# Softmax shift as the bias of eight exponentials a group, in the second and fourth of four cross-attentions

## The reference

```
L0: x = x + MHA(LN(x), LN(ctx)), 8 heads of 32; then a state scan over the 1024 rows (silu), plus a row of program weights
L1: attn = softmax(where(causal, q k^T / 8, -inf)), 16 heads of 64; x = attn v @ wo + bo + x
L2: scores = where(mask == 0, -1e9, q k^T / 4); e = exp(scores - max) * mask; probs = e / (sum e + 1e-9), 16 heads of 16
    x = LN(probs v @ Wo.T + bo + x)
L3: attn = softmax(where(xa_mask, -max_float, q k^T / 4)), 16 heads of 16; x = x + attn v @ proj; x = x + gelu(LN(x) @ fc1) @ fc2
```

## Time and profile before

| | |
|---|---|
| median of 3 runs | 1384.22 us (1378.32 to 1384.23) |
| the profiled execution | 1379.43 us, its span 1377.7 us |
| PE, PEld busy | 97%, 82% of the span |
| DVE, ACT, POOL busy | 66%, 49%, 41% of the span |

### The profile page before, as it was taken

One profiled execution on the slowest core, in us unless ns is written; L12 is line 12 of the kernel. 1 busy time (PEld: TensorE's weight loads), 2 busy tenths in 40 slices (PEclk: granted clock), 3 DMA queues, 4 the chain that ended last, 5 costly groups with the idle time before them and its releaser, 6 DMA issues.

```text
span 1377.7 us, 22993 instructions
## 1 busy us (share of the span) xinstructions
PE 1334.6 (97%) x8763; PEld 1123.6 (82%) x8763; DVE 902.5 (66%) x2204; ACT 676.7 (49%) x1497; POOL 558.7 (41%) x700
## 2 busy tenths in 40 slices
PE   6999999999999999999999999999999999899999
PEld 4889987777788788878888888779877887788778
DVE  4778772787755867575667556775677467746771
ACT  3667766134555453545444535446344643464444
POOL 4455432016613552454246311472156216621661
PEclk9999999999999999999999999999999999999999
DMA  5133502200000000000000001000000000000000
GB/s 148 39 82 124 165 24 81 62 10 1 1 16 16 1 9 9 16 1 9 1 9 1 24 4 30 0 1 13 19 1 1 17 16 1 1 5 12 1 1 16
DMA packets 48362, 34.10 MB, mean 25 GB/s; under 512 B 22076, under 2 KB 45435, under 8 KB 48251
## 3 DMA queue, kind: packets, MB, share of 16 engines
q1 hardware_dynamic: 46919, 32.44, 8.2%
q10 hardware_dynamic: 1332, 0.17, 0.1%
HBM read 23.26 MB, written 8.39 MB: 23 GB/s over the span
## 4 chain that ended last, share of the span: by engine, by line
PE 87%; DVE 5%; POOL 4%; ACT 2%; issue 1%; ACTq 0%; DMA 0%; SPq 0%; DVEq 0%
PE ps L886 11%; PE ps L876 10%; PE ps L836 10%; PE ps L855 8%; PE ps L932 8%; PE ps L943 8%; PE ps L846 6%; PE ps L896 6%; PE ps L802 5%; PE ps L785 5%; PE ps L1037 2%; PE ps L1050 1%; POOL pr L1607 1%; POOL pr L1621 1%; PE ps L924 1%; PE ps L905 1%
## 5 line engine op out<-in xcount | busy, mean ns | idle before, releaser
L1582 POOL TENSOR_TENSOR rstd<-mv,halfneg 128x1 f32<-128x1 f32 x192 | 107.5, 562 | 343.6 <-DVE mv L1317 342.3
L1163 ACT ACTIVATE pr<-pr 128x616 f32<-128x616 f32 x224 | 160.1, 716 | 167.5 <-DVE pr L1356 87.2
L1621 POOL TENSOR_TENSOR pr<-mx,pr 128x616 f32<-128x616 f32 x128 | 156.4, 1223 | 207.9 <-DVE mx L1351 207.2
L1167 ACT ACTIVATE pr<-ps 128x512 f32<-128x512 f32 x224 | 132.7, 596 | 157.3 <-PE ps L855 157.1
L855 PE MATMUL ps<-ident,pr 128*128 128x128 f32 (+1 forms) x1120 | 161.1, 277 | 8.3 <-ACT pr L1163 4.8
L886 PEld LDWEIGHTS ps<-vtab,pr 128*128 128x128 f32 (+1 forms) x1280 | 153.5, 191 | 13.2 <-ACT pr L1167 9.1
L886 PE MATMUL ps<-vtab,pr 128*128 128x102 f32 (+1 forms) x1280 | 161.2, 274 | 2.3 <-ACT pr L1167 1.1
L855 PEld LDWEIGHTS ps<-ident,pr 128*128 128x128 f32 (+1 forms) x1120 | 126.9, 140 | 35.1 <-ACT pr L1163 10.0
L876 PE MATMUL ps<-vwo,pr 128*128 128x256 f32 (+1 forms) x640 | 148.9, 381 | 0.0
L1415 DVE TENSOR_TENSOR xt<-xt,ps 128x256 f32<-128x256 f32 x192 | 79.7, 416 | 104.1 <-PE ps L896 48.4
L836 PE MATMUL ps<-wk,tt 128*128 128x308 f32 x512 | 145.2, 425 | 0.7 <-ACT tt L1142 0.7
(11 more groups left out here) (200 smaller groups left out, 2361.5 us busy)
## 6 DMA issues: line engine op xcount, KB each, us to landing
out_dram<-xt SPq DMA_DIRECT2D x64, 128.0 KB, 1.7
xt<-in_x_dram SPq DMA_DIRECT2D x32, 128.0 KB, 2.7
xt<-out_dram SPq DMA_DIRECT2D x32, 128.0 KB, 2.1
fc<-in_L_xattn_fc_w_dram SPq DMA_DIRECT2D x2, 1024.0 KB, 5.6
wk<-in_L_xattn_wkv_dram SPq DMA_DIRECT2D x4, 512.0 KB, 5.0
front<-in_L_xattn_wkv_dram SPq DMA_DIRECT2D x4, 512.0 KB, 6.5
wo<-in_L_xattn_wo_dram SPq DMA_DIRECT2D x1, 1024.0 KB, 5.2
kb<-in_L_xattn_wq_dram SPq DMA_DIRECT2D x1, 1024.0 KB, 5.1
```

The costliest lines, as they stand in the source:

```text
L1163: ac(v, v, ACT.Exp, scale=-ATTN[key[0]].scale).then_inc(done["expo"], 1)
L1167: ac(pr[:, run.lane, 0:4 * P], bank(run.lane, 0), ACT.Copy).then_inc(done["pturn_main"], 1)
L1582: p.tensor_tensor(rstd[:, n:n + 1], mv[:, n, 1:2], halfneg[:, :], ALU.pow).then_inc(done["rstd"], 1)
L1621: p.tensor_tensor(p8, mx[:, run.lane, :].unsqueeze(2).to_broadcast([P, HG, KEYS]), p8, ALU.subtract).then_inc(done["below"], 1)
```

## The change

In L1 and L3 the subtraction is gone as a step of its own. The tables of keys are stored negated and scaled (`wk_sb` and `k_sb` multiply by -1/8 and -1/4), the masks add a large positive number instead of a negative one, and `rowmax` takes the minimum of the negated scores. `expo` then does eight exponentials of 77 columns, one a head, exp(least - score), where `least` is a column of `mx` given as bias. In L1 each of the eight also writes the sum of its row to a new small buffer `total`, and `rowsum` is dropped. L1's exponential reads PSUM directly; L3's reads `pr`, in which `bound` has put the masked scores. L0 and L2 stay as they are, but for the line numbers.

```
+BY_HEAD = (L1, L3,)
...
-        steps += [("bound", k), ("rowmax", k), ("below", k)] if a in (L2, L3) else [("rowmax", k), ("shift", k)]
+        steps += [("bound", k)] * (a in (L2, L3)) + [("rowmax", k)]
+        if a not in BY_HEAD:
+            steps += [("below", k) if a in (L2, L3) else ("shift", k)]
         steps += [("expo", k)]
...
         if a is L1:
-            steps += [("rowsum", k), ("recip", k), ("weigh", k)]
+            steps += [("recip", k), ("weigh", k)]
...
             def expo(key, run):
-                s = "below" if key[0] in "23" else "shift"
+                a, lane = ATTN[key[0]], run.lane
+                if a in BY_HEAD:
+                    act.wait_ge(done["rowmax"], at("rowmax", key, run))
+                    src = score_view(lane) if a is L1 else heads_view(lane)
+                    for n in range(HG):
+                        least = mx[:, lane, n:n + 1]
+                        if a is L1:
+                            last = ac(heads_view(lane)[:, n, :], src[:, n, :], ACT.Exp, bias=least, scale=-1.0, accum_out=total[:, lane, n:n + 1])
+                        else:
+                            last = ac(heads_view(lane)[:, n, :], src[:, n, :], ACT.Exp, bias=least, scale=-1.0)
+                    last.then_inc(done["expo"], 1)
+                    return
...
-                v.tensor_reduce(mx[:, run.lane, :], src, AX.X, ALU.max).then_inc(done["rowmax"], 1)
+                v.tensor_reduce(mx[:, run.lane, :], src, AX.X, ALU.min if ATTN[key[0]] in BY_HEAD else ALU.max).then_inc(done["rowmax"], 1)
...
-            def rowsum(key, run):
...
-                s = {"1": "rowsum", "2": "den_eps"}.get(key[0], "mix")
+                s = {"1": "expo", "2": "den_eps"}.get(key[0], "mix")
...
-                    last = v.tensor_copy(o, src)
+                    last = v.tensor_scalar(o, src, -L1.scale, None, ALU.mult)
...
-                        last = v.tensor_tensor(kblk["3"][:, b, c, :, :], src, own, ALU.mult)
+                        last = v.scalar_tensor_tensor(kblk["3"][:, b, c, :, :], src, -L3.scale, own, ALU.mult, ALU.mult)
```

The strings of `TURNS` for PE, DVE, ACT and POOL are new from the start of the second phase on, without the dropped steps; the first phase and SyncE keep theirs. One piece of PE's, before and after:

```
-        "asasasaasaasaasaasaasaasaasaasasaasasasaasasasaasaasasaasaasasaaaaasaaaaasaaa0aa23s01011232030102121320303010120"
+        "asasasaasaasaasaasaasaasaasaasasaasasasaasasasaasaasasaasaasasaaaasaasaaaa0aaaaa201013s1232031010213230203012010"
```

More of the change, by code:

```diff
@@ L197 @@
     "scalar": ("item_act", "v0_lay", "turned", "query_bias", "expo", "pturn_main", "u_sb", "gelu", "w2_sb", "wqt_sb", "k1_sb", "vt_sb", "silu", "more_act"),
-    "vector": ("ctx_stats", "ctx_norm", "item_dve", "stats", "aggr", "norm", "bound", "rowmax", "shift", "rowsum", "den_eps", "recip", "weigh",
+    "vector": ("ctx_stats", "ctx_norm", "item_dve", "stats", "aggr", "norm", "bound", "rowmax", "shift", "den_eps", "recip", "weigh",
                "pturn_rest", "heads", "resid", "resume", "wk_sb", "vwo_sb", "k_sb", "v_sb", "carry", "ends", "gap", "agree"),
@@ L244 @@
[L244 to L248, removed]
@@ L260 @@
[L260 to L264, removed]
@@ L1159, in expo @@
             def expo(key, run):
-                s = "below" if key[0] in "23" else "shift"
+                a, lane = ATTN[key[0]], run.lane
[10 more added lines that the diff above has]
+                    return
+                s = "below" if a in (L2, L3) else "shift"
                 act.wait_ge(done[s], at(s, key, run))
-                v = pr[:, run.lane, 0:HG * KEYS]
-                ac(v, v, ACT.Exp, scale=-ATTN[key[0]].scale).then_inc(done["expo"], 1)
+                v = pr[:, lane, 0:HG * KEYS]
+                ac(v, v, ACT.Exp, scale=-a.scale).then_inc(done["expo"], 1)
             def pturn_main(key, run):
@@ L1343, in bound @@
                     off = out3[:, run.batch, run.tile:run.tile + 1, :].to_broadcast([P, HG, KEYS])
-                    last = v.scalar_tensor_tensor(heads_view(run.lane), off, NEG, score_view(run.lane), ALU.mult, ALU.add)
+                    last = v.scalar_tensor_tensor(heads_view(run.lane), off, -NEG, score_view(run.lane), ALU.mult, ALU.add)
                 last.then_inc(done["bound"], 1)
@@ L1356, in shift @@
                 v.tensor_tensor(heads_view(run.lane), top, score_view(run.lane), ALU.subtract).then_inc(done["shift"], 1)
-            def rowsum(key, run):
-                lane = run.lane
-                dve.wait_ge(done["expo"], at("expo", key, run))
-                v.tensor_reduce(mx[:, lane, :], pr[:, lane, 0:HG * KEYS].rearrange("p (h n) -> p h n", n=KEYS), AX.X, ALU.add)\
-                    .then_inc(done["rowsum"], 1)
             def mixed(key, lane):
@@ L1374, in recip @@
                 lane = run.lane
-                s = {"1": "rowsum", "2": "den_eps"}.get(key[0], "mix")
+                s = {"1": "expo", "2": "den_eps"}.get(key[0], "mix")
                 dve.wait_ge(done[s], at(s, key, run))
                 hd = ATTN[key[0]].hd
-                src = mixed(key, lane)[:, :, hd:hd + 1].rearrange("p h o -> p (h o)") if s == "mix" else mx[:, lane, :]
+                src = mixed(key, lane)[:, :, hd:hd + 1].rearrange("p h o -> p (h o)") if s == "mix" else mx[:, lane, :] if s == "den_eps" else total[:, lane, :]
                 v.reciprocal(rec[:, lane, :], src).then_inc(done["recip"], 1)
@@ L1500, in _ @@
             steps = {"ctx_stats": ctx_stats, "ctx_norm": do_ctx_norm, "item_dve": item_dve, "stats": stats, "aggr": aggr, "norm": norm, "bound": bound, "rowmax": rowmax,
-                     "shift": shift, "rowsum": rowsum, "den_eps": den_eps, "recip": recip, "weigh": weigh,
+                     "shift": shift, "den_eps": den_eps, "recip": recip, "weigh": weigh,
                      "pturn_rest": pturn_rest, "heads": heads, "resid": resid, "resume": resume, "wk_sb": wk_sb, "vwo_sb": vwo_sb, "k_sb": k_sb,
@@ L1568, in zeros @@
                 made(p.memset(causal[:, :, :], 0.0))
-                made(p.affine_select(out=causal[:, 0, :], in_=causal[:, 0, :], compare_op=ALU.is_ge, fill=NEG, base=0,
+                made(p.affine_select(out=causal[:, 0, :], in_=causal[:, 0, :], compare_op=ALU.is_ge, fill=-NEG, base=0,
                                      pattern=[[-1, KEYS]], channel_multiplier=1))
```

76 lines of the change are left out of this document (43 added, 33 removed).

## The result

| | median us | range | runs | ratio to before, 95% interval |
|---|---|---|---|---|
| before | 1384.16 | 1378.32 to 1384.23 | 4 | |
| changed | 1393.13 | 1387.95 to 1395.07 | 4 | 1.0068 (1.0043 to 1.0092) |

The forecast was 1374 us. The changed kernel is about 9 us slower. The profiled executions say the same: 1379.43 us before, 1387.95 after.

A forecast was written before the change was run, and what follows sets the result against it. Matmul issue was taken as the bound, 87% of the chain, with TensorE short of work in L2/L3. Terms -10, -3 and +3 gave -10 us on the profiled 1379.43, so 1369.4, or 1374 us as median; range 1350 to 1404.

The forecast's parts named there:

- (a): GpSimd's queue in the starved stretches: without L3's below, 19% off GpSimd's 55 us on the chain, -10 us.
- (b): VectorE loses 11% of its work, mostly off the chain in L1: 4% of its 69 us, -3 us.
- the starved stretches: Windows 1020 to 1060 and 1150 to 1200 us, lanes in L2 and L3: TensorE short of work, GpSimd and VectorE near 80%.
- (c): ScalarE's 28 us on the chain grow with L3's added load, L1's being hidden behind matmuls: +3 us.
- TensorE's new order I count at nothing: TensorE's changed order of steps costs or gains nothing, since its work and the lanes' spacing are the same.
- The second, ScalarE in GpSimd's place in L3: Rival: in L3, lanes wait for ScalarE, 2.55 us a group against TensorE's 2.36, eating (a): 1384 us; chance 0.19.
- The third: Rival: copies and turned steps queue behind ScalarE's runs of eight, +12 us: 1396 us; chance 0.13.
- The fourth: Rival: L1's row sums are serial, 4.8 us for eight; ScalarE becomes the bound in L1: 1412 us; chance 0.15.
- The first: Rival: more is won in the starved stretches, GpSimd's chain part falls by half (-28 us): about 1356 us; chance 0.15.
- The chance for slower: Whole kernel more than about 0.5%, 7 us, slower: the third and fourth rivals together, 0.28.
- ScalarE's share of the chain reaches GpSimd's old 4%: Sign of being wrong in the changed profile; ScalarE's chain share was forecast at not over 3%.
- The stretches at 1020 and 1150 us: Sign of being right: in these windows GpSimd at 65 to 70% busy and TensorE's chain share up.

The follow-up runs named there:

- e4: e1 with L1's exponentials writing no row sums and rowsum back on VectorE; 1421.50 us, ratio to before 1.0290.
- e7: Kernel before, its order, with one minimum and one biased exponential per group in L1 and L3; shift and below gone, rowsum kept; 1383.18 us.
- e9: Changed kernel, its own order, with one biased exponential per group in L1 and L3 and no row sums in L1; 1381.26 us, ratio to before 0.9971.
- e10: e7 with L2's rowmax and below also left out, so L2's exponential takes unshifted scores; 1380.51 us, ratio to before 0.9982.
- e13: Kernel before without L2's offset step of the layer norm on GpSimd; 1384.44 us, ratio to before 0.9994.
- e8: Changed kernel, its own order, with one minimum and one biased exponential per group in L3 only; 1385.75 us, ratio to before 1.0003.
- e1: Changed kernel's steps in the order of the kernel before, with the turns of dropped steps taken out; 1433.16 us, ratio to before 1.0351.
- e6: Kernel before, all steps and order kept, with L1's and L3's exponentials cut into eight, L1's with unread sums; 1547.25 us, ratio to before 1.1177.

## Why the prediction was wrong, point by point

**The prices were nearly right.** L3's run was put at 1.95 us, within 2.07, and is 2.10; L1's at 3.0 and is 2.56; ScalarE at about 900 us and is 866. Eight of 77 columns out of PSUM were put at 1.83 and are 1.84 in e4. Reading SBUF, one exponential follows another after (2.10 - 0.35) / 7 = 0.25 us; reading PSUM, after (1.84 - 0.35) / 7 = 0.21. The prediction had allowed 0.03 us for SBUF and the trace shows 0.04. The estimate from the figures of the Trainium skill, page "ScalarE: Activation LUTs", section "What ACT_TABLE_LOAD costs", is 0.251 us and 2.10 for eight. For SBUF the trace agrees, for PSUM it doesn't.

**The first step that failed is (a), -10 us for GpSimd's queue, with (b), -3 for VectorE.** Both took a share of the chain as time that shrinks with the load. Where 13 us were forecast, relief alone is worth 1.5 us in the old order (e7, 129 us of steps gone, not distinguishable from nothing) and 4 in the new (e9, 179 us gone). Twice e7's relief gives 0.2% (e10), and a step on the chain itself gives nothing (e13). The chain says through which steps the last result came. It does not say that the next best way is any shorter. GpSimd's 80% in the starved stretches was not what starved them: at 57% and 46% (e10) the kernel is at most 0.4% shorter. The same holds the other way: ScalarE's 11% of the chain are 152 us, of which its runs cost 13.

**The second is (c), +3 us for ScalarE, too small by 10.** L3's runs cost 9 us, and L1's, which were counted as hidden behind matmuls, 4 (e8, e9). The terms forecast were -13 + 3, the measured ones are -4 + 4 + 9 = +9, so about half of the miss lies in each step. The measured terms are differences along one row of kernels, so they must add up to the result; each is uncertain by some 3 us. Either step alone, put right, would have given about no change; it takes both to get the sign.

**"TensorE's new order I count at nothing" hid the largest number.** The steps alone, in the order that was there, cost 49 us (e1); the new order brought 40 back. I looked at the order only for the lanes' spacing, and had no term for how well an order fits the lengths of its steps. That the forecast missed by 19 us and not by 60 is owed to an order about which it said nothing: luck.

**The rivals.** The second, ScalarE in GpSimd's place in L3, describes what the timeline shows at 1333 us, and its price of +10 over my forecast was for L3 alone; L3's measured cost is 9. It comes nearest in mechanism, though (a), which it was to eat, was never there. The third gave 1396 and came nearest in time. Its mechanism, copies that stand behind a run, seems to be at most a small part: for L1167's copies TensorE waited 13 us before the change, for the same copies (L1189) 14 after, while its wait for exponentials rose from 14.9 us to 24.9, 18.0 of them for L3's. What a run makes another lane's exponential wait was not taken apart. The fourth did not occur: the reads are pipelined. The first was excluded by e7 and e10. The chance for slower, 0.28, was too low mainly because (a) was taken for granted.

**The signs I had named.** "ScalarE's share of the chain reaches GpSimd's old 4%" came true with 11%. The stretches at 1020 and 1150 us did relax as forecast, GpSimd to 72% and 67%, and the time rose all the same.

**What stays open.** What limits TensorE in the starved stretches is not settled: GpSimd's load and VectorE's are worth a few us, one step of the norm nothing. My guess, that with an order fixed for all engines each lane waits for turns of the others rather than for its own work, was not tried, since it needs an order made anew for e7's or e10's steps. Orders mixed from both kernels, one engine's new and another's old, were not tried either, so which engine's order brings the 40 us is open. Nor was a version found that beats both kernels by more than a few us: e10's 1380.5 has an interval that reaches to no change. Its shortest and its longest runs are each some 3 to 4 us under those of before (1375.0 against 1378.0, 1382.0 against 1385.9), but it gives up the subtraction in L2.

## What to carry to other kernels

Where every engine's order is fixed by hand or by a planner, ask first whether the order is made anew for the new lengths: here that was worth 40 us, the change itself 9. Read the chain for where the time passes, not for how much can be won; a removal experiment of the suspected step is the test. And eight small activations in place of one added 1.4 to 1.8 us a group on an engine that looked half idle. That came to 13 us of the time in an order made for them, and with no relief elsewhere, in an order not made for them, to 163.

## What the runs showed of the hardware

A row sum taken along with an exponential is a second instruction on ScalarE. It lengthens the distance from one 77-column exponential out of PSUM to the next from 0.21 us (eight in 1.84, e4) to 0.30 (1257.03 to 1257.33 in the changed kernel).

Part of the spread between runs of one kernel is TensorE's granted clock near the start. Windows of the changed kernel's profile, then of e8's, both from 0 to 50 us; the last three columns are granted clock, DMA share and GB/s:

```profile
0.00:50.00 50.00, 38.16 (x254) 31.25 (x254) 25.77 (x75) 22.32 (x58) 22.37 (x65) 0.97 0.43 107
```

```profile
0.00:50.00 50.00, 38.58 (x206) 30.97 (x207) 22.00 (x64) 18.74 (x48) 19.12 (x60) 0.86 0.44 103
```

With a mean of 0.97 of 2.4 GHz TensorE got through 254 matmuls in the first 50 us, with 0.86, that is a longer stretch at 1.2 GHz, through 206. Over a whole run that is a mean clock of 0.998 against 0.994, and the changed kernel took 1387.95 us in the one run at 0.998 and 1392.61 to 1395.07 in the three at 0.994. The kernel with the most waiting, e6, had a mean clock of 0.979, with 0.96 in a window in its middle, where the changed kernel shows 1.00:

```profile
640.00:680.00 40.00, 33.62 (x191) 26.47 (x190) 26.07 (x56) 21.78 (x84) 17.81 (x20) 0.96 0.00 1
```

What TensorE did before and after one fall in that window of e6 (668 to 674, 674 to 676 and 676 to 680 us):

```profile
668.00:674.00 6.00, 6.00 (x40) 4.30 (x38) 4.38 (x9) 2.66 (x7) 5.34 (x7) 1.00 0.00 0
674.00:676.00 2.00, 0.38 (x4) 0.00 (x0) 1.94 (x3) 2.00 (x9) 1.78 (x2) 1.00 0.02 4
676.00:680.00 4.00, 3.81 (x20) 3.77 (x21) 1.28 (x3) 2.11 (x7) 1.98 (x2) 0.57 0.00 0
```

It was busy 0.38 of 2 us while ScalarE was busy throughout, and in the 4 us that follow its mean clock is 0.57, most of them at 1.2 GHz. So in the kernels with the most waiting a part of the loss can be TensorE falling to 1.2 GHz after it had waited; no run takes this apart. For e1 an estimate: its profiled execution has a mean clock of 0.989 against 0.994 in most runs of before, which would be about 0.005 x 1433 = 7 us; its other four have 0.992 to 0.994, so in those it is under 3 of the 49.
